# Row sums of the softmax: weights of a chunk's sets added up on VectorE, one set of ones-matmuls per chunk

## What is computed

```python
xn = layernorm(x)
x = x + attention(xn) + ffn(xn)
# attention: q, k, v = xn @ Wq.T, xn @ Wk.T, xn @ Wv.T, 16 heads of 32, q and k rotated (rope)
#   scores = q @ k.T / sqrt(32), causal; pattern = softmax(scores); (pattern @ v) @ Wo.T
# ffn: (silu(xn @ Wg.T) * (xn @ Wu.T)) @ Wd.T; hidden width 2048 in layer 0, 1408 in layer 1
#   (layer 1 has scales on the three products)
```

## Time and profile before

| | |
|---|---|
| time, median of 3 runs | 2245.01 us (2243.44 to 2249.74) |
| the profiled execution | 2243.66 us, its span 2241.8 us |
| TensorE busy | 2034.9 us (91%) |
| VectorE busy | 1176.1 us (52%) |
| ScalarE busy | 737.9 us (33%) |
| GpSimd busy | 760.3 us (34%) |
| mean granted TensorE clock | 0.978 |

### The profile page before, as it was taken

The page is one execution under the profiler, slowest core; times in us unless marked ns, Lnnn a source line. Parts: engine busy times, 40 slices in busy tenths (PEclk is TensorE's granted clock), DMA queues, the critical chain, the costliest instruction groups (busy, mean ns, idle before and its releaser), DMA issues.

```text
span 2241.8 us, 34912 instructions
## 1 busy us (share of the span) xinstructions
PE 2034.9 (91%) x10176; PEld 1352.9 (60%) x10176; DVE 1176.1 (52%) x2458; ACT 737.9 (33%) x1357; POOL 760.3 (34%) x552
## 2 busy tenths in 40 slices
PE   4999999999899999999869999999997999999996
PEld 3756657566475646476557576674755746464764
DVE  5635637355555646374357265472736537282733
ACT  2242332423323342423322423324242242415242
POOL 3324324242321515153323143431423215142523
PEclk9999999999899999999979999999998999999998
DMA  3313103041130303041123041220411303030403
GB/s 136 79 32 95 43 28 94 15 114 43 38 74 28 89 19 98 10 118 30 53 103 96 11 104 33 54 83 9 113 34 43 85 11 98 10 98 17 126 24 122
DMA packets 72428, 140.67 MB, mean 63 GB/s; under 512 B 9328, under 2 KB 26736, under 8 KB 71152
## 3 DMA queue, kind: packets, MB, share of 16 engines
q1 hardware_dynamic: 72304, 139.25, 22.2%
HBM read 75.77 MB, written 4.19 MB: 36 GB/s over the span
## 4 chain that ended last, share of the span: by engine, by line
PE 44%; issue 26%; POOL 15%; DVE 6%; ACT 2%; SPq 2%; DMA 2%; DVEq 1%; POOLq 1%; ACTq 1%
PE D L900 10%; PE G L900 8%; PE S L969 7%; PE O L986 6%; PE U L900 6%; PE E L993 3%; POOL pr L745 3%; POOL swapped L727 3%; POOL pr L733 2%; ACT pr L639 2%; POOL wgl L698 2%; POOL hl L721 2%; SPq L576 2%; POOL wul L698 1%; PE S L953 1%
## 5 line engine op out<-in xcount | busy, mean ns | idle before, releaser
L639 ACT ACTIVATE pr<-S 128x512 f32<-128x512 f32 (+3 forms) x768 | 341.1, 489 | 293.7 <-PE S L969 292.0
L868 DVE TENSOR_TENSOR xres<-D,xres 128x512 f32<-128x512 f32 x352 | 242.2, 688 | 347.4 <-PE D L900 341.3
L721 POOL TENSOR_TENSOR hl<-tt,hh 128x512 fp32r<-128x512 f32 x108 | 138.9, 1286 | 550.2 <-ACT hh L663 550.0
L969 PE MATMUL S<-QS,KS 98*128 98x512 f32 (+2 forms) x768 | 240.5, 388 | 11.4 <-DMA QS<-mt 5.7
L969 PEld LDWEIGHTS S<-QS,KS 98*128 98x128 f32 x768 | 132.8, 188 | 192.1 <-ACT pr L639 171.0
L663 ACT CAST hh<-tt 128x512 fp32r<-128x512 f32 x108 | 67.0, 620 | 481.8 <-DVE tt L882 481.8
L745 POOL TENSOR_SCALAR_AFFINE_SELECT pr<-pr 128x512 f32<-128x512 f32 x128 | 81.2, 635 | 379.7 <-ACT pr L639 379.7
L986 PE MATMUL O<-pr,vh 128*32 128x512 f32 (+3 forms) x1536 | 163.8, 498 | 46.4 <-POOL pr L745 45.5
L858 DVE RECIPROCAL denom<-denom 128x256 f32<-128x256 f32 x64 | 109.1, 1730 | 181.0 <-ACT denom L646 181.0
L900 PE MATMUL G<-xh,wgh 128*128 128x512 f32 x432 | 177.6, 411 | 14.2 <-DVE tt L879 10.6
L900 PE MATMUL D<-wdh,hh 128*128 128x512 f32 x432 | 180.1, 417 | 4.1 <-DVE xres L868 3.2
(11 more groups left out here) (137 smaller groups left out, 3737.6 us busy)
## 6 DMA issues: line engine op xcount, KB each, us to landing
KS<-pr SPq DMA_DIRECT2D x192, 128.0 KB, 2.3
QS<-pr SPq DMA_DIRECT2D x192, 128.0 KB, 2.3
raw<-in_wgate_dram SPq DMA_DIRECT2D x29, 512.0 KB, 3.5
raw<-in_wup_dram SPq DMA_DIRECT2D x28, 512.0 KB, 3.7
raw<-in_wdown_dram SPq DMA_DIRECT2D x28, 512.0 KB, 3.4
raw<-in_wqk_dram SPq DMA_DIRECT2D x18, 512.0 KB, 3.4
vh<-val SPq DMA_DIRECT2D x16, 512.0 KB, 3.8
val<-in_x_dram SPq DMA_DIRECT2D x6, 1024.0 KB, 10.3
```

Source lines behind the costliest of these rows:

```text
L639: act.activation(pr[:, (i * HG + h) % 8, skip:W], S[h % 2][:, skip:W], ACT.Exp, scale=SCALE) \
L721: pool.tensor_tensor(hl[:, fc, :], tt[:, (blk * nfc + fc) % 2, :], hh[:, fc, :].bitcast(F32), ALU.subtract) \
L868: dve.tensor_tensor(xres[:, rt, :], d[:, :], xres[:, rt, :], ALU.add).then_inc(sem["v_dfree"], 1)
L969: pe.matmul(S[h % 2][:, first:W], KS[0:SHIFT, h, kb * P:(kb + 1) * P], QS[0:SHIFT, h, c * W + first:(c + 1) * W], start=True, stop=True).t ...
```

## The change

VectorE gets a step `acc`: it adds the unnormalised weights of a set to a tile `acc` (4 heads of 512 columns) as soon as they are complete. Set 0 is written into `acc` itself by ScalarE; set 4, the first of chunk 1, is copied into it. The step stands behind `pv` of the same set. The step `sums` is issued once per chunk, full width, from `acc`, and waits for the last `acc`. ScalarE's exp now waits for three semaphores: the scores, `pv` of the set before the last one, and `acc` of that set. `swapped` and `xn` become parts of `acc`.

```diff
@@ -94,10 +94,12 @@
         scores = [("st", i, h) for h in range(HG)] if i < len(SETS) else []
         if i < len(SETS) and diagonal(i):
             scores.append(("causal", i))
-        now = [scores[:2] + [("pv", i - 1)], scores[2:] + [("sums", i - 1)]]
+        now = [scores[:2] + [("pv", i - 1)], scores[2:]]
+        if i > 1:
+            now[0].append(("acc", i - 1))
         c, kb = SETS[i - 1]
         if kb == TPC * (c + 1) - 1:
-            now[-1].append(("heads", c))
+            now[-1] += [("sums", c), ("heads", c)]
         st.append(now)
     return st
 
@@ -234,8 +236,9 @@
     "shift": {"v_chain": 2, "v_m": 1, "p_shift": 1, "v_shift": 1, "d_shift": 32},
     "st": {"p_st": 1, "a_exp": 1},
     "causal": {"g_causal": 1},
-    "pv": {},
-    "sums": {"p_pv": 1},
+    "pv": {"p_pv": 1},
+    "acc": {"v_acc": 1},
+    "sums": {"p_sums": 1},
     "heads": {"a_heads": 1},
     "recip": {"v_recip": 1},
     "scaled": {"v_heads": 1, "a_ah": 1, "g_al": 1},
@@ -415,7 +418,8 @@
         QS, KS = sb("QS", [P, HG, T], F32R), sb("KS", [P, HG, T], F32R)
         wvh = QS[:, 0:2, :].rearrange("p a (b n) -> p (a b) n", n=D)
         wvl = QS[:, 2:4, :].rearrange("p a (b n) -> p (a b) n", n=D)
-        swapped = sb("swapped", [P, 2, W])
+        acc = sb("acc", [P, HG, W])
+        swapped, xn = acc[:, 0:2, :], acc[:, 2:4, :]
 
         trig = sb("trig", [P, 2, T])
         wv_raw = trig[:, :, :].rearrange("p a (b n) -> p (a b) n", n=D)
@@ -423,7 +427,6 @@
         pr = sb("pr", [P, 8, W])
         flat_h = [pr[:, 2 * NC * k:2 * NC * k + NC, :].rearrange("p c n -> p (c n)") for k in range(2)]
         flat_l = [pr[:, 2 * NC * k + NC:2 * NC * (k + 1), :].rearrange("p c n -> p (c n)") for k in range(2)]
-        xn = sb("xn", [P, 2, D])
         heads, denom = sb("heads", [P, W]), sb("denom", [P, W])
         ah, al = sb("ah", [P, W], F32R), sb("al", [P, W], F32R)
         tt = sb("tt", [P, 2, W])
@@ -511,6 +514,10 @@
             at = n.turns * (2 * PAIRS[1]) + (2 * j + fc)
             return bass.ds(at, 1)
 
+        def weights(i):
+
+            return pr[:, i * HG % 8:i * HG % 8 + HG, :] if i else acc
+
         def proj_bank(n, t):
 
             return S[t % 2] if n.region[:4] == "open" else NB[t]
@@ -635,12 +642,17 @@
                 c, kb = SETS[i]
                 skip = max(0, kb - TPC * c) * P
                 act.wait_ge(sem["p_st"], n("p_st", 1))
-                act.wait_ge(sem["p_pv"], n("p_pv"))
-                act.activation(pr[:, (i * HG + h) % 8, skip:W], S[h % 2][:, skip:W], ACT.Exp, scale=SCALE) \
+                later = -1 if h >= 2 else 0
+                act.wait_ge(sem["p_pv"], n("p_pv", later if i else 0))
+                if i:
+                    act.wait_ge(sem["v_acc"], n("v_acc", later if i > 1 else 0))
+                else:
+                    act.wait_ge(sem["p_sums"], n("p_sums"))
+                act.activation(weights(i)[:, h, skip:W], S[h % 2][:, skip:W], ACT.Exp, scale=SCALE) \
                     .then_inc(sem["a_exp"], 1)
 
             def heads_(n, c):
-                act.wait_ge(sem["p_pv"], n("p_pv"))
+                act.wait_ge(sem["p_sums"], n("p_sums"))
                 act.wait_ge(sem["g_al"], n("g_al"))
                 act.copy(heads[:, :], O[:, :])
                 act.copy(denom[:, :], E[:, :]).then_inc(sem["a_heads"], 1)
@@ -741,7 +753,7 @@
                 skip = (kb - TPC * c) * P
                 pool.wait_ge(sem["a_exp"], n("a_exp"))
                 pool.sem_inc(s_seen, 1)
-                blocks = pr[:, i * HG % 8:i * HG % 8 + HG, skip:skip + P]
+                blocks = weights(i)[:, :, skip:skip + P]
                 pool.affine_select(out=blocks, in_=blocks, pattern=[[0, HG], [1, P]], compare_op=ALU.is_ge, fill=0.0,
                                    base=0, channel_multiplier=-1).then_inc(sem["g_causal"], 1)
 
@@ -852,6 +864,23 @@
                 dve.wait_ge(sem["p_shift"], n("p_shift", 1))
                 dve.tensor_copy(mt[:, :], E[0:2 * HG * RT, 0:P]).then_inc(sem["v_shift"], 1)
 
+            def accumulate(n, i):
+                c, kb = SETS[i]
+                skip = max(0, kb - TPC * c) * P
+                if diagonal(i):
+                    dve.wait_ge(sem["g_causal"], n("g_causal"))
+                dve.wait_ge(sem["a_exp"], n("a_exp", -2 if i < len(SETS) - 1 else 0))
+                if i == 1:
+                    dve.wait_ge(sem["p_pv"], n("p_pv", -1))
+                total_, now = acc[:, :, skip:W], weights(i)[:, :, skip:W]
+                if kb:
+                    dve.wait_ge(sem["v_acc"], n("v_acc"))
+                    ins = dve.tensor_tensor(total_, total_, now, ALU.add)
+                else:
+                    dve.wait_ge(sem["p_sums"], n("p_sums"))
+                    ins = dve.tensor_copy(total_, now)
+                ins.then_inc(sem["v_acc"], 1)
+
             def recip(n, c, k):
                 dve.wait_ge(sem["a_heads"], n("a_heads"))
                 half = slice(k * W // 2, (k + 1) * W // 2)
@@ -882,7 +911,7 @@
                 dve.scalar_tensor_tensor(t, t, both_s[:, chunk(n, j, fc)] if n.layer else 0.5, U[:, :],
                                          ALU.mult, ALU.mult).then_inc(sem["v_h"], 1)
 
-            walk(dve, dict(v_weights=v_weights, stats=stats, xn=xn_, norm=norm, proj=proj, rotate=rotate, nat=nat, shift=shift,
+            walk(dve, dict(acc=accumulate, v_weights=v_weights, stats=stats, xn=xn_, norm=norm, proj=proj, rotate=rotate, nat=nat, shift=shift,
                            recip=recip, scaled=scaled, add_wo=add_wo, add_down=add_down, gated=gated))
 
 
@@ -983,16 +1012,15 @@
                 else:
                     pe.wait_ge(sem["a_exp"], n("a_exp", -2))
                 for h in range(HG):
-                    pe.matmul(O[h * DH:(h + 1) * DH, skip:W], vh[:, kb, h * DH:(h + 1) * DH],
-                              pr[:, (i * HG + h) % 8, skip:W], start=kb == 0, stop=kb == TPC * (c + 1) - 1)
-
-            def sums(n, i):
-                c, kb = SETS[i]
-                skip = max(0, kb - TPC * c) * P
+                    ins = pe.matmul(O[h * DH:(h + 1) * DH, skip:W], vh[:, kb, h * DH:(h + 1) * DH],
+                                    weights(i)[:, h, skip:W], start=kb == 0, stop=kb == TPC * (c + 1) - 1)
+                ins.then_inc(sem["p_pv"], 1)
+
+            def sums(n, c):
+                pe.wait_ge(sem["v_acc"], n("v_acc"))
                 for h in range(HG):
-                    ins = pe.matmul(E[h * DH:(h + 1) * DH, skip:W], ones[:, :], pr[:, (i * HG + h) % 8, skip:W],
-                                    start=kb == 0, stop=kb == TPC * (c + 1) - 1)
-                ins.then_inc(sem["p_pv"], 1)
+                    ins = pe.matmul(E[h * DH:(h + 1) * DH, :], ones[:, :], acc[:, h, :], start=True, stop=True)
+                ins.then_inc(sem["p_sums"], 1)
 
             def wo_(n, c, i):
                 if c == 0 and i == 0:
```

## The result

The changed kernel takes 2383.4 us (median of 4 runs, 2381.71 to 2383.9); the kernel before took 2244.23 on the same chip. The ratio is 1.062 [1.059, 1.064], so it is slower by some 139 us. The profiled execution took 2381.71 us, with a span of 2379.9. The direction was forecast, the size was not: +40 was forecast.

A forecast was written before the change was run, and what follows sets the result against it. TensorE, busy for 91% of the span, was taken as the bound, with waits deciding what its removed work gains. Turn1 +54, turn0 -13, tail0 +5 and tail1 -6 gave +40 us on 2245.01: forecast 2284 us, range 2228 to 2315.

The forecast's parts named there:

- the sum: Whole kernel: turn1 +54, turn0 -13, tail0 +5, tail1 -6 us, together +40 us.
- VectorE's durations: VectorE's additions: 2.3, 1.8, 1.2 and 0.7 us by width, 1.22 for the copy; 17.8 us a turn.
- Turn1's stall: Turn1, second chunk: reciprocals queue behind set 5's addition, delaying the heads' cast and exponentials; TensorE idle 5.75 us, output steps +3.65.
- The third wait: Each exponential waits for three semaphores, not two: 1.75 us in turn1, 1.2 in turn0, 1.6 in tail0, 1.0 in tail1.
- The clock: Half-speed TensorE: 1.7 us behind turn1's stall, 0.7 at its second chunk's thinner end, 0.8 in tail0; bounds nothing and twice.
- Rival 3: Worse, 2308 us, chance 0.15: masks held by additions, or another clock fall in thinned diagonal sets, 1.7 us in 14 turns.
- Rival 3's other half: Dense diagonal sets: GpSimd masks held by VectorE additions, some 1.7 us a turn in 14 turns; within the rival's 0.15.
- Saved steps: Sums steps taken off TensorE's path: turn0 -3.4 us and tail1 -3.9 us before the third wait.
- Tail0: Set 5's addition between the reciprocals delays heads about 1.2 us, saved steps offset; +0.3, with wait and clock +2.7 us.
- TensorE's busy time: Sign to look for across the whole run: TensorE busy about 120 us less.

The follow-up runs named there:

- e2: Changed kernel with turn1's addition of set 5 moved from ahead of the reciprocals to behind the scaling of the heads; 2339.71 us, ratio 1.042.
- e5: Kernel before with a third wait for each exponential, on a semaphore that has long been reached; 2266.57 us, ratio 1.0085.
- e6: Changed kernel without the exponentials' wait for pv, so each has two waits as before; 2346.78 us, ratio 1.045.
- e4: Changed kernel without additions and third wait; one full sums step per chunk, from its last set's weights alone; 2281.76 us, ratio 1.014.
- e7: Changed kernel without additions and third wait, sums from the last set alone, old diagonal sums steps issued again and overwritten; 2236.86 us, ratio 0.996.
- run 45: Not a run label: the words "in all of the run 45 us (e9)" mean e9 took 45 us less than the changed kernel.
- e9: Changed kernel with the old sums steps of the eight diagonal sets of a turn issued again, results overwritten; 2338.22 us, ratio 1.042.
- e8: Changed kernel with turn1's set 5 addition behind the scaled heads, no exponential wait for pv, old diagonal sums issued again; 2262.69 us, ratio 1.008.
- e3: Changed kernel with additions and copy over 128 columns a head, the other columns left out; 2365.81 us, ratio 1.053.
- hybrid: Kernel before with additions only for sets 5 to 7 in turn0 and tail1, one full sums step replacing four; 2219.83 us, ratio 0.988.

## Why the prediction came out as it did

The direction and the main stall were right; the sum of +40 us was 99 short. Two steps of it failed, each by about 39 us: the clock in the stretches of diagonal sets, which was put at nothing for stretch A, and the saved steps net of the additions, which were overdrawn. Two more terms were too small, the stall by 12 and the third wait by 14. The four add up to 104, since single gains overlap by some 5.

- **VectorE's durations: right.** Estimated 2.3, 1.8, 1.2, 0.7 and 1.22 us for the copy. The profile has means of 2.37, 1.80, 1.23, 0.69 and 1.22.
- **Turn1's stall: right in mechanism and place**, 5.63 us idle against 5.75. Its price with the slow stretch behind it was 3.65 + 1.7 us a turn, 32 us in six turns; e2 gave 44 back.
- **The third wait: right for the kernel before**, too small for the changed one. The sum had 1.75, 1.2, 1.6 and 1.0 us a turn, 23 us in all; e5 gives 14 to 24, e6 gave 37 back.
- **The clock: the first step that failed.** The sum had 16 us for it, 10 of them behind turn1's stall and 6 elsewhere, and its upper bound was twice that. The text says of the diagonal chain that taking the sums step out "only makes the idle time longer". That is so, and I priced longer idle time at nothing. The 128 diagonal steps were free on the path, but they were part of what kept TensorE busy there; without them the chain itself runs at half clock. In stretch A that is about 2.1 us of the 2.9 to 3.7 us in each turn (e4 minus e7: 1.92, 1.82, 2.36 and 1.74 us; 33 us over 16 turns), and in all of the run 45 us (e9), where the sum had 6 outside the stall.
- **The rest of stretch A** is accounted for too: one full step more at the end, 0.75 us (e7), and the third wait, 0.4 to 1.2 us (A in the trace of e5). With the clock's part they add up to 2.9 to 3.9 us.
- **Rival 3 was the better account**, though its 2308 us are 75 short as well. It had the mechanism, a stretch of diagonal sets that is thinner for its lost sums, at 1.7 us a turn. I held against it that turn1's dense stretch ran at 1.00 throughout. That was the wrong evidence, since that row was taken with the sums steps in it. What would have warned was a row of a diagonal stretch with their time taken off. In the one of turn0 above there are four sums steps; the first three, which go, last 1.06, 0.85 and 0.64 us, so of 10.52 us busy in 11.50 about 8 remain. The earlier trace rows has a fall behind 1.67 us busy of 3.40, which is thinner still, so the two rows together could raise a doubt but not settle it. Rival 3's other half, masks held by additions, did not occur in the changed kernel: none of the 128 masks overlaps an addition, and their mean is 634 ns (before 635).
- **Saved steps: the second step that failed.** What the sum had outside the stall, the third wait and the clock comes to -21 us; e8, with those three cured, is 18 us above the kernel before. For turn0 I had -3.4 us. The steps without any addition and with a full clock give 1.85 less in B and 0.74 more in A (e7). In turn1 four full steps less give next to nothing: in e7 TensorE waits 0.61 us for the exponentials between two sets, and a set takes 3.24 us where it took 3.32. On top come the additions, 26 us (e8 minus e7), of which the sum had only some 0.5 us at the end of each turn1 and 1.2 us in each tail0. (The twelve steps of a turn are 11.9 us by the prediction's own prices, not 11.8; that changes nothing.)
- **Tail0: wrong by 7 us a turn.** +2.7 was forecast and 9.6 measured. I had weighed the contention between VectorE and GpSimd for the masks and for tail1, and not for `al` in tail0, which comes exactly when VectorE, done with the scaled heads, starts an addition. It doubled to 2.52 us, TensorE waited 3.46, and its clock fell behind that. With short additions 5.2 us of it are gone from B (e3).
- **TensorE's busy time.** 120 us less was expected and 12 more came. It measures clock as well as work, and so it couldn't serve as a sign of the work removed.

By region the miss is 42 us in turn1 (16.0 a turn against 8.95), 25 in turn0 (+2.0 against -2.2), 14 in tail0 and 17 in tail1 (+5.5 against -2.9). A region is counted here up to the first scores of the next; 2.2 us of turn1's 16.0 lie behind the copy of the second heads, where the half clock goes on (5.6 us a turn, before 0.4).

## What to carry to other kernels

Matmuls that are off the path in a chain bound by latency need not be free to remove. Take their time off the busy time of the stretch and compare that with stretches of the same trace behind which the clock fell. That is a warning and no proof; the cheap test is e4, the kernel with nothing but the removal. Work that moves to another engine is paid at three more places: what is queued behind it there (44 us here), the waits that it adds to every instruction (37, by themselves 14 to 24), and the other engine that it contends with (a part of the 15 us that e3 gave back in the tails). Take it only where TensorE is bound and filler stands around, as the hybrid does.

## What the runs showed of the hardware

- TensorE's clock fell to 0.50 in stretches without any wait over about 0.5 us (e4), when TensorE had been busy for 2.21 of 3.40 and part of the next 3.30 us; filling the waits with matmuls whose result is overwritten brought it back to 1.00 there and took 45 us off, with and without additions.
- A wait that is always fulfilled, in front of each exponential, costs 14 to 24 us of 2244 (e5); the time from one narrow exponential to the next goes from 0.31 us before to 0.43 in e5 and 0.45 in the changed kernel.
- A GpSimd product with SBUF inputs that started during a VectorE addition with two SBUF inputs made hardly any progress until that ended (2.52 instead of 1.29 us), and an addition that started second took 3.11 instead of 2.29.
- Shortening a wait need not shorten the stretch: with 1.6 us less of stall in each turn1 (e3), the time at half clock there rose by 4.0 us and the stretch stayed at 39.1 us.
